# A graph-attention and three-layer GCN kernel: GpSimd waits once per attention batch, ahead of its third group of four row gathers

## The chip, the cores and the metric

The kernel runs on one core of one Trainium2 chip. The metric is the device time of one execution in microseconds (us), and a smaller number is better. Before the change it is 5381.48 us, the median of three runs.

## What is computed

The graph has 6250 nodes with 128 features and 106,250 edges, sorted by destination. Everything is float32. First comes one heterogeneous graph-attention layer with 8 heads of 16 features, 4 node types and 6 edge types. Cut to what matters here:

```python
k, q, v = (typed_linear(x, W, ntype) for W in (Wk, Wq, Wv))     # by node type
kw = typed_rel(k[src], rel_att, etype)                          # by edge type
a  = (kw * q[dst]).sum(-1) * rel_pri.T[etype] / sqrt(16)
m  = typed_rel(v[src], rel_msg, etype)
ex = exp(a - segment_max(a, dst)[dst])
h  = segment_sum(m * (ex / segment_sum(ex, dst)[dst]), dst)     # then Wa, gate, layer norm
```

Three GCN layers follow, each of which sums h[src] * norm over the edges of a destination, with a batch norm behind it, and a last residual and layer norm.

## The kernel before

**Tables.** Because the key and message of an edge depend only on its source node and its edge type, the kernel first writes a table `kv_tab` to HBM with one row per node and edge type: 37,500 rows of 256 floats (1 KB), the key half and the message half. This takes the first 420 us or so.

**Attention batches.** The edges are then handled in 52 batches (`NB`) of 16 tiles (`TPB`) of 128 edges. A batch has four groups (`NG`) of four tiles (`GRP`). GpSimd fetches the rows of a tile with one indirect DMA, `G.indirect_dma_start(kv[b % 3][:, t, :], ...)` at L528, which brings 128 rows of 1 KB (128 KB). So a batch takes 16 gathers, issued one behind the other by the loop in `gather(b)`. The rows land in one of three buffers, `kv[b % 3]`, and each group of four gathers has its own semaphore, `kv_land[b % 3][g]`, which is at 64 * (b // 3 + 1) when all four have landed.

The work on a batch is spread over the engines, written out in a fixed order by hand:

- TensorE takes the query rows of each tile by a one-hot matrix product (`q_rows`, L866; it signals `q_done` per group). For the batch one behind it, it runs a few tiny products that carry the segment maximum from tile to tile (`chain_f` L890, `spread_f` L894, `chain_b` L898, `spread_b` L902), and the weighted sums over the edges of a tile (`aggregate`, L881 and L884).
- VectorE multiplies keys and queries (`products`, L1228, which waits for `kv_land` and for `q_done`), reduces them to logits (L1235), runs the scans of the segment maximum (`max_1` to `max_5`; L1264 is the first instruction of `max_2` and waits for `chain_f`; L1269 waits for `spread_f`), multiplies messages and weights (`weigh`, L1307, which signals `vw_ready` per group), and adds the sums of TensorE to the accumulators in SBUF (L1330).
- ScalarE builds the one-hot matrices (L646, L650, L658, L661; L646 waits for `q_done` of a group two back) and takes the exponentials.
- In each of batches 1 to 34 SyncE also writes two or three blocks of zeros of 1.8 MB into a dense matrix `a_tab` in HBM (`feed`, L423), at the time of the gathers of the batch one further on.

**What paces GpSimd.** The rows of batch b take the place of batch b - 3. So `gather(b)` waits, group by group, for `vw_ready` of batch b - 3: `pool.wait_ge(vw_ready, NG * (b - 3) + g + 1)`. TensorE, VectorE and ScalarE are working on batch b - 1 or b - 2 at that time. Besides the gathers GpSimd issues scatters of single words into `a_tab` (`scatter`, L485), which are spread over the batches by `slots`: none in some, two in others, and nine in each batch from number 37 on. From batch 3 on each batch therefore shows as one burst of GpSimd DMAs. Behind the last batch GpSimd issues 48 more scatters in a row (`SY`).

**GCN layers.** In each layer GpSimd gathers rows of 512 bytes (L557) in groups of four into a ring of four groups, and before a group it waits for `sum_done`, a signal of TensorE's sums (L998), while TensorE multiplies the dense part (L1021).

Of the kernel before, what the change touches and what calls it, by code (L numbers as in the profile page):

```python
# [62 lines left out]
def gnn(nc, x, src, dst, etype, ew, ntype, Wk, Wq, Wv, Wa, rel_pri, rel_att, rel_msg, skip, gamma, beta,  # L63
# [50 lines left out]
    with ExitStack() as ctx:  # L114
# [3 lines left out]
        def sem(name):  # L118
            return ctx.enter_context(nc.semaphore(name))
# [137 lines left out]
        kv_land = [[sem(f"kv_land{a}_{g}") for g in range(NG)] for a in range(3)]  # L257
# [199 lines left out]
        def _(pool):  # L457
# [26 lines left out]
            def scatter(t):  # L484
                G.indirect_dma_start(a_tab, bass.IndirectOffsetOnAxis(cell[:, t:t + 1], 0), tot[:, t:t + 1], None)\  # L485
                 .then_inc(cells_saved, 16)
# [17 lines left out]
            for j in range(ZC - 1, NCH - 1):  # L504
                b = 2 if j < ZC else next(b for b in range(NB) if zeros_by(b) >= BPC * (j + 1)) + 3
# [8 lines left out]
            def gather(b):  # L514
                pool.wait_ge(idx_ready, b + 1)
                pool.sem_inc(gathers_begun, 1)
                if b == 2:
                    pool.wait_ge(tot_ready, 1)
                for g in range(NG):
                    for t, j in slots.get((b, g), ()):  # L520
                        pool.wait_ge(a_zeroed[j], 16 * BPC)
                        scatter(t)
                    if b >= 3:
                        pool.wait_ge(vw_ready, NG * (b - 3) + g + 1)
                        pool.sem_inc(gathers_begun, 1)
                    for s in range(GRP):
                        t = g * GRP + s
                        G.indirect_dma_start(kv[b % 3][:, t, :], None, kv_tab,  # L528
                                             bass.IndirectOffsetOnAxis(idxr[:, b % 3, t:t + 1], 0))\
                         .then_inc(kv_land[b % 3][g], 16)  # L530
            for b in range(NB):
                gather(b)
# [1098 lines left out]
```

## Time and profile before

| | |
|---|---|
| time, median of three runs | 5381.48 us (5376.69 to 5386.73) |
| the profiled execution: span from first to last instruction | 5345.2 us, 57754 instructions |
| the profiled execution's own time | not listed; the median of the runs is 36.3 us above its span |
| busy share PE / PEld / DVE / ACT / POOL | 72% / 49% / 44% / 21% / 49% |
| attention batches, start of the gathers to start of the last burst | 422.8 to 2555.7 us |
| mean granted TensorE clock | 0.832 of full speed |
| gathers of attention: POOL L528 | x832, 808.5 us busy, mean 972 ns |
| before them POOL idle | 889.4 us, 64 times, on DVE L1307 |

How to read it: times are microseconds from the first instruction. PE is TensorE's matmuls, PEld its weight loads, DVE VectorE, ACT ScalarE, POOL GpSimd, SP SyncE; POOL's span of an indirect DMA is the time in which it makes the descriptors, not the time in which the rows move. In a row of the timeline the bracket holds the time for which the engine sat idle before the instruction, and what ended it. "remote" is an event that the profile can't put to an instruction that has just ended, and "issue" is idle time in which the engine waited for nothing that the profile shows.

### The profile page before, as it was taken

Reading aid. Unit: us, or ns where it says so; the run is one execution under the profiler, and the core shown is the slowest. Engines: PE = TensorE matmul, PEld = TensorE weight load, DVE = VectorE, ACT = ScalarE, POOL = GpSimd, SP = SyncE. Lnnn points to the kernel's source line nnn. Section 1 sums busy time; section 2 is a strip of 40 time slices with the busy share of each in tenths; the row PEclk is TensorE's granted clock in tenths of the full one; section 3 lists DMA queues with packets and bytes.
Section 4 is the critical chain, followed back from the end, with each engine's and each line's share of the span. In section 5 each row is a group of like instructions: output and inputs, shape, how many; then the busy total and the mean of one; then the engine's idle time right before and its main releaser. Section 6 shows DMA issues by size and latency. Waiting matters only on the chain. (4 is left out here: it accounts for less than half of the span.)

```text
span 5345.2 us, 57754 instructions
## 1 busy us (share of the span) xinstructions
PE 3871.6 (72%) x17006; PEld 2627.4 (49%) x17006; DVE 2374.6 (44%) x8260; ACT 1139.1 (21%) x2513; POOL 2613.5 (49%) x2753
## 2 busy tenths in 40 slices
PE   5883666666666655555362889999889899889996
PEld 4662555555555544444330544444544445445453
DVE  4552444444544433433264354334454335454336
ACT  1222444544444433333211100000000000000001
POOL 0004344344443455445533466665566665666663
PEclk9996777776777666666575999999999999999998
DMA  7994445444454322112001566767677677767774
GB/s 170 380 396 152 181 156 182 145 172 166 148 188 147 106 61 59 56 52 63 22 25 55 204 252 260 273 254 273 254 261 266 254 268 265 265 252 267 269 268 153
DMA packets 265570, 1020.69 MB, mean 191 GB/s; under 512 B 66086, under 2 KB 114373, under 8 KB 227632
## 3 DMA queue, kind: packets, MB, share of 16 engines
q1 hardware_dynamic: 132060, 716.86, 35.7%
q0 software_dynamic: 102352, 248.59, 14.4%
q10 hardware_dynamic: 30852, 51.55, 2.8%
q8 instruction: 145, 2.38, 0.2%
q14 instruction: 161, 1.32, 0.1%
HBM read 797.16 MB, written 219.61 MB: 190 GB/s over the span
## 5 line engine op out<-in xcount | busy, mean ns | idle before, releaser
L557 POOL DMA_INDIRECT stage<-h_tab,earr x1536 | 1454.3, 947 | 879.9 <-issue 425.1
L1021 PE MATMUL bank<-arena,xr 128*128 128x512 f32 (+1 forms) x3822 | 1748.3, 600 | 57.6 <-issue 54.6
L528 POOL DMA_INDIRECT arena<-kv_tab,idxr x832 | 808.5, 972 | 1161.1 <-DVE arena L1307 889.4
L1021 PEld LDWEIGHTS bank<-arena,xr 128*128 128x128 f32 x3822 | 707.8, 194 | 808.3 <-issue 808.0
L1540 DVE TENSOR_TENSOR sums<-sums,bank 128x128 f32 x1536 | 437.2, 285 | 907.2 <-remote 706.4
L881 PE MATMUL bank<-oh,stage 128*128 128x128 f32 x1664 | 408.7, 371 | 341.2 <-issue 337.2
L1511 DVE TENSOR_SCALAR oh<-iota_j,earr 128x128 f32<-128x128 f32 x1536 | 557.6, 370 | 96.8 <-DVE sums L1531 29.8
L998 PEld LDWEIGHTS bank<-oh,stage 128*128 128x128 f32 x3072 | 398.2, 193 | 333.1 <-issue 332.2
L881 PEld LDWEIGHTS bank<-oh,stage 128*128 128x128 f32 x1664 | 338.4, 272 | 423.7 <-issue 422.1
L884 PE MATMUL bank<-oh,arena 128*128 128x128 f32 x1664 | 380.3, 367 | 196.2 <-issue 189.0
L646 ACT ACTIVATE arena<-arena,iota_p 128x512 f32<-128x512 bf16 x416 | 276.2, 712 | 1137.8 <-remote 1049.0
L866 PE MATMUL bank<-xr,arena 128*128 x3328 | 460.6, 300 | 69.3 <-issue 40.7
L998 PE MATMUL bank<-oh,stage 128*128 128x128 f32 x3072 | 424.1, 280 | 113.7 <-issue 112.5
L712 ACT ACTIVATE rs<-mv,epsc 128x49 f32<-128x49 f32 (+1 forms) x6 | 1.9, 316 | 2314.8 <-DVE mv L1583 2120.9
L866 PEld LDWEIGHTS bank<-xr,arena 128*128 128x128 f32 x3328 | 443.6, 216 | 75.5 <-issue 74.1
L884 PEld LDWEIGHTS bank<-oh,arena 128*128 128x128 f32 x1664 | 326.3, 272 | 224.5 <-issue 224.4
L1330 DVE TENSOR_TENSOR sums<-sums,bank 128x256 f32 x832 | 347.8, 418 | 57.0 <-DVE sums L1330 11.8
L485 POOL DMA_INDIRECT a_tab<-tot,cell x320 | 310.4, 970 | 100.1 <-issue 99.8
L1228 DVE TENSOR_TENSOR arena<-arena,bank 128x512 f32<-128x512 f32 x208 | 142.3, 684 | 486.1 <-remote 408.0
L658 ACT ACTIVATE oh<-iota_j,earr 128x128 f32<-128x128 f32 x832 | 262.6, 386 | 57.8 <-remote 52.6
L1264 DVE COPY negall<-bank 8x16 f32<-8x16 f32 x52 | 8.4, 162 | 599.5 <-remote 576.0
L650 ACT ACTIVATE arena<-arena,epsc 128x512 f32<-128x512 f32 x416 | 274.6, 708 | 0.0
(217 smaller groups left out, 2887.6 us busy)
## 6 DMA issues: line engine op xcount, KB each, us to landing
arena<-a_tab SPq DMA_DIRECT2D x273, 1792.0 KB
a_tab<-stage SPq DMA_DIRECT2D x70, 1792.0 KB
a_tab<-sums POOLq DMA_DIRECT2D x21, 1792.0 KB, 13.4
kv_tab<-stage SPq DMA_DIRECT2D x48, 768.0 KB
arena<-rel_d SPq DMA_DIRECT2D x52, 512.0 KB
stage<-h_tab,earr POOLq DMA_INDIRECT x1536
arena<-key_d ACTq DMA_DIRECT2D x40, 512.0 KB, 10.7
arena<-in_edge_weight ACTq DMA_DIRECT2D x40, 512.0 KB, 13.4
```

Of the source, the lines that this page charges most:

```text
L485: G.indirect_dma_start(a_tab, bass.IndirectOffsetOnAxis(cell[:, t:t + 1], 0), tot[:, t:t + 1], None)\
L528: G.indirect_dma_start(kv[b % 3][:, t, :], None, kv_tab, bass.IndirectOffsetOnAxis(idxr[:, b % 3, t:t + 1], 0))\
L557: G.indirect_dma_start(gring[:, (q % NG) * GRP + s, :], None, h_tab[l], bass.IndirectOffsetOnAxis(src_i[:, t:t + 1], 0)).then_inc(row_land ...
L646: al.inc(S.activation(ohT[k][:, g % 2, :], relb[:, par, g * GRP * P:(g + 1) * GRP * P], ACT.Abs, scale=-1.0, bias=iota_p[:, k:k + 1]))
L866: last = M.matmul(bank[g % 2][:, s * D:(s + 1) * D], ohT[k][:, g % 2, s * P:(s + 1) * P], xr[:, k:NT - 1 + k, :][:, bass.ds(blocks[s], 1), ...
L881: M.matmul(o_[s][:, P:2 * P], exw[:, g * GRP + s, :], oh[:, g, s, :], start=True, stop=True)
L884: last = M.matmul(o_[s][:, 0:P], vw[:, g * GRP + s, :], oh[:, g, s, :], start=True, stop=True)
L998: last = M.matmul(bank[q % NG][:, s * P:(s + 1) * P], gring[:, (q % NG) * GRP + s, :], oh[:, q % NG, s, :], start=True, stop=True)
L1021: mm = M.matmul(o_[:, 0:cw], xr[:, n, :], abuf[B % NBUF][:, n % KB, 0:cw], start=n == 0, stop=n == NT - 1)
L1330: V.tensor_tensor(w_, w_, d_.rearrange("p (k j) -> p k j", k=2), ALU.add).then_inc(acc_added, 1)
L1511: V.tensor_scalar(oh[:, q % NG, s, :], iota_j[:, :], rel_c[:, t:t + 1], ew_c[:, t:t + 1], ALU.is_equal, ALU.mult).then_inc(wt_ready, 1)
L1540: V.tensor_tensor(w_, w_, bank[q % NG][:, s * P:(s + 1) * P], ALU.add).then_inc(win_added, 1)
```

## The change

One wait is added in `gather(b)`, on GpSimd. In every batch, when it comes to the third group of gathers (g == 2), GpSimd waits until the four gathers of the second group of the same batch have landed. The wait stands ahead of the scatters and of the `vw_ready` wait of that group. All instructions, their order and their sizes stay as they are.

```diff
@@ -517,6 +517,8 @@
                 if b == 2:
                     pool.wait_ge(tot_ready, 1)
                 for g in range(NG):
+                    if g == 2:
+                        pool.wait_ge(kv_land[b % 3][g - 1], 64 * (b // 3 + 1))
                     for t, j in slots.get((b, g), ()):
                         pool.wait_ge(a_zeroed[j], 16 * BPC)
                         scatter(t)
```

## Rows read from the trace of the kernel before

**Rows 1.** Page, part 2: DMA share in 40 slices of the span.
```profile
DMA  7994445444454322112001566767677677767774
```

**Rows 2.** Waits, 515 to 2606 us: total us, times, longest us.
```profile
ACT arena L646 <- remote: 992.3, 91, 21.4
POOL arena L528 <- DVE arena L1307: 889.4, 64, 29.9
DVE negall L1264 <- remote: 502.7, 43, 21.0
...
PEld bank L881 <- issue: 417.6, 468, 2.7
```

**Rows 3.** Timeline of POOL: starts (and two ends) of bursts; start, us.
```profile
515.05 0.94 POOL L528 DMA_INDIRECT arena<-kv_tab,idxr  x1 [29.89 <-DVE arena L1307]
...
594.33 0.94 POOL L528 DMA_INDIRECT arena<-kv_tab,idxr  x1 [18.41 <-DVE arena L1307]
632.21 0.94 POOL L528 DMA_INDIRECT arena<-kv_tab,idxr  x1 [17.81 <-DVE arena L1307]
...
1700.29 0.94 POOL L528 DMA_INDIRECT arena<-kv_tab,idxr  x1 [17.72 <-DVE arena L1307]
...
1722.02 0.95 POOL L528 DMA_INDIRECT arena<-kv_tab,idxr  x1 [0.30 <-issue]
1740.91 0.94 POOL L528 DMA_INDIRECT arena<-kv_tab,idxr  x1 [17.94 <-DVE arena L1307]
...
2063.96 0.99 POOL L528 DMA_INDIRECT arena<-kv_tab,idxr  x1 [16.95 <-DVE arena L1307]
...
2094.76 0.96 POOL L485 DMA_INDIRECT a_tab<-tot,cell  x1 [0.30 <-issue]
...
2113.37 0.99 POOL L528 DMA_INDIRECT arena<-kv_tab,idxr  x1 [17.65 <-DVE arena L1307]
...
2555.68 0.99 POOL L528 DMA_INDIRECT arena<-kv_tab,idxr  x1 [17.48 <-DVE arena L1307]
```

**Rows 4.** Timeline of the batch whose burst starts at 1700.29.
```profile
1704.57 3.65 PEld L866 LDWEIGHTS bank<-xr,arena 128*128 128x128 f32 x32
...
1714.75 0.69 DVE L1228 TENSOR_TENSOR arena<-arena,bank 128x512 f32<-128x512 f32 x1 [7.39 <-remote]
...
1726.17 0.16 DVE L1264 COPY negall<-bank 8x16 f32<-8x16 f32 x1 [9.80 <-remote]
...
1731.80 0.18 DVE L1269 TENSOR_TENSOR tmp<-bank,tsel 128x16 f32<-128x16 f32 x1 [3.31 <-PE bank L894]
...
1733.67 0.23 PE L898 MATMUL bank<-rhs,hsel 128*8 128x32 f32 x2
```

**Rows 5.** Timeline of the first burst, batches 0 to 2.
```profile
431.60 0.95 POOL L528 DMA_INDIRECT arena<-kv_tab,idxr  x1 [0.30 <-issue]
...
439.37 0.69 DVE L1228 TENSOR_TENSOR arena<-arena,bank 128x512 f32<-128x512 f32 x1 [2.46 <-DMA arena<-kv_tab,idxr]
...
441.02 2.05 PE L866 MATMUL bank<-xr,arena 128*128 x16 [0.37 <-issue]
...
473.37 1.33 ACT L646 ACTIVATE arena<-arena,iota_p 128x512 f32<-128x512 bf16 x2 [36.02 <-remote]
```

**Rows 6.** Timeline of the last batches, VectorE, no gathers left.
```profile
2662.25 1.29 DVE L1307 TENSOR_TENSOR arena<-arena,stage 128x512 f32<-128x512 f32 x2 [0.17 <-ACT stage L677]
...
2685.17 1.29 DVE L1307 TENSOR_TENSOR arena<-arena,stage 128x512 f32<-128x512 f32 x2 [0.16 <-ACT stage L677]
```

**Rows 7.** Timeline of POOL in a GCN layer, behind twelve gathers.
```profile
3513.63 0.94 POOL L557 DMA_INDIRECT stage<-h_tab,earr  x1 [2.57 <-remote]
```

**Rows 8.** Windows, two bursts: us, busy PE, PEld, DVE, ACT, POOL; PEclk, DMA share, GB/s.
```profile
1700.29:1722.96 22.67, 12.53 (x80) 11.37 (x79) 7.99 (x20) 6.04 (x11) 17.49 (x18) 0.73 0.77 276
...
2063.96:2095.72 31.76, 15.02 (x86) 12.82 (x85) 7.96 (x20) 5.84 (x11) 24.45 (x25) 0.66 0.30 87
```

**Rows 9.** Waits of POOL: total us, times, longest us.
```profile
POOL stage L557 <- remote: 291.9, 125, 3.8
```

## The prediction

> **What bounds the kernel now.** I read the slices of the page first. The attention batches fill the stretch from about 423 to 2700 us, and there no engine and no DMA queue is full: the DMA share is 0.4 to 0.5 while zeros are written and 0.1 to 0.2 later [rows 1]. So some chain of waits must set the pace, and the list of waits names its members: ScalarE, VectorE and GpSimd all wait, and TensorE's L881 sits idle 468 times in front of one instruction on "issue" [rows 2].
>
> The timeline of GpSimd shows the pattern. Each batch is a burst of DMAs 1.25 us apart and then some 18 us in which GpSimd waits for `weigh`. The length of a batch is burst plus a constant. A batch with 16 DMAs takes 632.21 - 594.33 = 37.9 us, one with 18 takes 40.6 us, one with 25 takes 49.4 us [rows 3]: 9 more DMAs at 1.28 us make 11.5 us more, all of it paid. Yet the gathers are for a batch that nobody needs soon. So the burst is serial with the attention work, although no data ties them.
>
> The timeline of one batch shows where. The query products (L866, begun at 1704.57, half of them done by 1706.5) free L1228 and L646 only at 1714.7. L1264 is let go only at 1726.17, which is 3.2 us behind the end of the burst (1722.97) [rows 3, 4]. The first burst, of three batches, is plainer: the products at 437 to 440.7 let ScalarE go at 473.37, with TensorE empty in between [rows 5]. What TensorE has done becomes visible late while GpSimd issues DMAs back to back, and TensorE itself then steps on in single instructions. Bandwidth is not the reason: in the burst at 2063.96 the DMA share is 0.30, in the one at 1700.29 it is 0.77, and the constant behind the burst is about the same, 17.65 and 17.94 us [rows 3, 8]. Without GpSimd's DMAs a batch takes 2685.17 - 2662.25 = 22.9 us [rows 6]. I call this the backlog, without a claim on what it consists of. It begins some 6 us into a burst (the products of 1704.57 are the first work caught) and ends some 3 us behind its end. Which part of the chip does it, these rows do not tell.
>
> The page "TensorE: Matmul & The Clock Gate" of the Trainium skill (the paragraph on engine queue depths) gives TensorE a queue of 64 instructions. By that rule work could run ahead by 64 before TensorE itself stumbles, and the trace has it get through the 32 loads and 32 products of L866 at full speed first [rows 4]. Nothing below needs this.
>
> **The change, part by part.** It adds one wait, no instruction with a duration, and moves nothing in order. Queued behind it on GpSimd are the scatters and eight gathers of groups 2 and 3 (11.3 us in an 18-DMA batch) and then the next batch; who waits for those is `products` of two batches on, which has over a period of slack, so the late landing of groups 2 and 3 costs nothing (the cover is some 40 us, the delay under 7). SyncE's queue is not touched.
>
> The pause, step one, its price. GpSimd's own pause costs g', the landing time of group 1 less the 0.3 us of idle that stands before a gather anyway. No wait of this kind is in the trace. From below: in the GCN layers a pause between two gathers lasts 2.57 - 0.30 = 2.3 us by its row [rows 7]; it ends with a signal of TensorE, not with a landing. The mean of 125 such pauses is 291.9 / 125 = 2.3 us with those 0.3 in it [rows 9], so 2.0 us is the lower end. From above: the second group of the very first batch was issued by 432.55 and its rows were seen at 439.37 [rows 5], 6.8 us, so 6.5 us, with 1.8 MB blocks of zeros ahead of it in GpSimd's own queue. In the bursts with SyncE's zeros (batches 3 to 35, 33 of them) I take 4.0 us, between the ends, since those zeros are in another queue. In the 15 further periods the DMA share is 0.30 [rows 8] and I take 2.0 us, with 2.9 us as the upper end (the 3.2 us from a burst's end to the release of L1264, less 0.3).
>
> "DMA: Bandwidth & Descriptors" of the Trainium skill ("Anatomy of one DMA") gives a GpSimd DMA about 2.0 us plus bytes over 436 GB/s, which would be 2.3 us for 128 KB; an estimate by that page would be a g' of 2.0 us throughout.
>
> Step two, what the pause frees. Behind it the backlog should end, as it ends behind each burst, and what TensorE had done by then becomes visible: L1228, and some 2 us later L1264 (my estimate: L1228 itself and two like it stand before it, 0.7 us each [rows 4]). From there the chain runs at full speed, until GpSimd has again issued for some 6 us. L1264 to L1269 takes 1731.80 - 1726.17 = 5.6 us [rows 4], with 2 us before it 7.6 us, so I expect the backlog of the second half to catch the release of L1269. It is held until 3.2 us behind the end of the second half. What is then left to the next burst is 1740.91 - 1731.80 = 9.1 us, where now it is 1740.91 - 1726.17 = 14.7 us [rows 3, 4]. A batch was 22.7 + 3.2 + 14.7 = 40.6 us; it will be 22.7 + g' + 3.2 + 9.1, a change of g' - 5.6 us.
>
> Sum: 33 x (4.0 - 5.6) = -52.8 us and 15 x (2.0 - 5.6) = -54 us, together -106.8 us. The first burst and the last one, with its 48 scatters, pay a pause and win a little; I put them at nothing (within 5 us). The GCN layers are not touched. The span goes from 5345.2 to 5238 us, and with the 36.3 us by which the median of the runs stands above it, the time to 5275 us, 2.0% less. With the upper g' in all, the change is 33 x 0.9 - 15 x 2.7 = -11 us; with the lower one 48 x -3.6 = -173 us. So this case reaches from 5208 to 5371 us.
>
> **The rivals.**
> A, slower: the pause does not clear the backlog. The place is the restart of GpSimd. All pauses that I see end with a signal of TensorE, that is after the state has ended; the new one ends with a DMA, and may end sooner. Then L1264 still waits for the end of the whole burst and the pause comes on top: 33 x 4.0 + 15 x 2.0 = +162 us, 5543 us (48 x 2.0 = +96 us, 5477 us, to 33 x 6.5 + 15 x 2.9 = +258 us, 5639 us). It decides where g' is shorter than what ends the state, some 3 us, or g' above 5.6 us for any reason. For it: 2.0 is under 3. Against it: a burst's end and a landing are nearly one event, and the first half has the zeros to make g' longer.
>
> "Rules for kernel authors" on that page, "DMA: Bandwidth & Descriptors" of the Trainium skill, say to issue DMAs early and wait on their semaphore late, so that the fixed cost overlaps. The wait here stands right behind the issue; by that rule nothing is won and each pause is exposed. No run here shows it yet.
>
> B, no change: the two cancel, when g' is near its upper end in the zeroing batches. 5370 to 5392 us.
>
> C, more: the backlog of the second half comes later, or the chain gets there sooner. If L1269 passes and L898's result (1733.67, 2.1 us later with 7.2 us left [rows 4]) is the first caught, each batch wins 1.9 us more: 48 x 1.9 = 91 us, 5184 us, with the low g' 5117 us. If nothing of the second half is caught, a batch is 11.3 us (first half) + 3 + 2 + 14.7 = 31.0 us in place of 40.6: 48 x -9.6 = -461 us, 4920 us. For it: a second half of 8 gathers is 10 us, of which only 4 are slow. Against it: in the bursts now, work done 6 us in was already 8 us late [rows 4].
>
> **How the numbers follow.** Main case 0.50 (of it 0.01 within the bound of no change), A 0.20, B 0.07, C with L898 0.15, C in full 0.08. A measurement of this kernel can tell 0.2% (11 us) from no change: the three runs lie within 10 us. Faster 0.49 + 0.15 + 0.08 = 0.72, same 0.01 + 0.07 = 0.08, slower 0.20. The predicted time is that of the main case, 5275 us; its own range is 5208 to 5371 us. For 8 in 10 the range takes in the lower C and B, and the near edge of A: 5110 to 5480 us (0.50 + 0.15 + 0.07 + some 0.06). Outside are the full C and most of A.
>
> **What would show it.** In the timeline of POOL each burst falls in two halves of 8 gathers, with an idle of 2.3 to 7 us between them put down to a DMA or to remote; its mean over 52 batches is g' + 0.3. If the main case holds, L1264 sits some 15 us behind the start of the burst and no longer 3 us behind its end, its wait of 502.7 us [rows 2] falls to under 250 us, a new wait of 5 us or more stands before L1269, and GpSimd's wait for L1307 falls from 17.7 to about 12 us. If L1264 stays 3 us behind the burst's end and GpSimd's wait stays at 17.7, it is A. If bursts follow each other in 31 us, it is C in full. The prediction is wrong in its base if the backlog hangs on something other than GpSimd's back-to-back issue, for instance on how many DMAs a batch has in all.

## The result and the profile after

The changed kernel takes 5132.88 us, the median of four runs (5121.71 to 5159.32). The kernel before, timed beside it, takes 5379.08 us (5375.12 to 5386.73). The ratio is 0.9548, 95% interval 0.9521 to 0.9576: 246 us less, where 106 us less was forecast. The direction was right and the time lies in the range of 5110 to 5480 us, near its lower end and below the main case's own range of 5208 to 5371 us.

The profiled execution of after has a span of 5120.0 us and took 5121.71 us, so a time is its span and 1.7 us. The 36.3 us which the forecast put around the span of before were therefore not around it: that profiled execution took about 5347 us, less than each of the four runs timed beside after. A second profile of the kernel before, taken later, has a span of 5379.4 us.

Lines that stand behind the new wait have moved by two: L528 is L530 now, L1264 is L1266, L1269 is L1271, L1307 is L1309. The page of after:

```profile
PE 3800.9 (74%) x17006; PEld 2582.1 (50%) x17006; DVE 2370.9 (46%) x8260; ACT 1140.0 (22%) x2513; POOL 2613.6 (51%) x2753
...
L530 POOL DMA_INDIRECT arena<-kv_tab,idxr x832 | 809.0, 972 | 889.2 <-DVE arena L1309 396.0
```

and the gathers on the page of before:

```profile
L528 POOL DMA_INDIRECT arena<-kv_tab,idxr x832 | 808.5, 972 | 1161.1 <-DVE arena L1307 889.4
```

The work is the same as before, and the gathers take as long as they did. All idle time in front of them fell from 1161.1 to 889.2 us, 271.9 us less. The part of it spent on `weigh` (L1307, now L1309) fell from 889.4 to 396.0 us, and a part of what was saved there is taken by the new wait.

The attention batches in two windows, first of after and then of before. Columns: us, then busy us and instructions of PE, PEld, DVE, ACT, POOL, then the granted clock, DMA share and GB/s. The first window of each holds the 33 periods with SyncE's zeros (batches 3 to 35), the second the 15 behind them:

```profile
507.63:1628.54 1120.91, 747.13 (x4687) 686.04 (x4687) 609.92 (x1651) 607.85 (x1354) 550.07 (x567) 0.78 0.55 192
1628.54:2311.57 683.03, 403.19 (x2132) 358.94 (x2132) 277.25 (x751) 279.19 (x616) 364.73 (x374) 0.68 0.21 61
```
```profile
515.05:1819.75 1304.70, 820.51 (x4688) 740.34 (x4688) 608.47 (x1651) 609.44 (x1354) 549.50 (x567) 0.72 0.46 165
1819.75:2555.68 735.93, 400.94 (x2132) 348.10 (x2132) 276.12 (x751) 276.59 (x616) 364.76 (x374) 0.67 0.20 57
```

The 33 zeroing periods went from 1304.70 / 33 = 39.54 us to 1120.91 / 33 = 33.97 us, 5.6 us each and 183.8 us in all. The 15 others went from 49.06 to 45.54 us, 3.5 us each and 52.9 us in all. The start of batch 3 comes 7.4 us sooner. What lies behind the start of the last burst is 5120.0 - 2311.57 = 2808.4 us long against 5345.2 - 2555.68 = 2789.5 us, 18.9 us more. So 183.8 + 52.9 + 7.4 - 18.9 = 225.2 us, which is the difference of the spans. The 18.9 us are no effect of the change: in a second pair of profiles, both from one chip (Q below), the last part is 2802.1 us after and 2810.7 us before. On that pair the periods went from 39.58 to 33.99 us and from 49.69 to 46.22 us, again 5.6 and 3.5 us.

Waits of after, 500 to 2460 us: total us, times, longest us.

```profile
ACT arena L648 <- remote: 500.4, 52, 21.3
POOL arena L530 <- DVE arena L1309: 396.0, 57, 18.6
...
DVE tmp L1271 <- remote: 220.1, 16, 58.2
POOL arena L530 <- DMA arena<-kv_tab,idxr: 202.8, 29, 7.7
...
DVE negall L1266 <- remote: 125.8, 18, 14.3
```

ScalarE's wait for TensorE has halved from 992.3 us, and VectorE's wait at L1266 (L1264 before) is down from 502.7 to 125.8 us [rows 2]. The new wait shows as a DMA that lets L530 go: 29 times, 202.8 / 29 = 7.0 us each. Where a scatter stands first behind it, it is put down to L485 instead, and where it is short, to "issue".

One late batch of after, POOL first and then VectorE:

```profile
2129.26 0.99 POOL L530 DMA_INDIRECT arena<-kv_tab,idxr  x1 [12.14 <-DVE arena L1309]
...
2141.00 0.94 POOL L530 DMA_INDIRECT arena<-kv_tab,idxr  x1 [0.30 <-issue]
2144.00 0.97 POOL L485 DMA_INDIRECT a_tab<-tot,cell  x1 [2.06 <-DMA arena<-kv_tab,idxr]
...
2161.81 0.95 POOL L485 DMA_INDIRECT a_tab<-tot,cell  x1 [0.30 <-issue]
2174.87 0.99 POOL L530 DMA_INDIRECT arena<-kv_tab,idxr  x1 [12.10 <-DVE arena L1309]
...
2143.85 0.69 DVE L1230 TENSOR_TENSOR arena<-arena,bank 128x512 f32<-128x512 f32 x1 [7.56 <-remote]
...
2165.69 0.17 DVE L1271 TENSOR_TENSOR tmp<-bank,tsel 128x16 f32<-128x16 f32 x1 [13.57 <-remote]
```

The last gather of the first half ends at 2141.94 and L1230, which waited since 2136.3 for products that TensorE had ended by 2137.8, is let go at 2143.85, 1.9 us later and inside the pause. The second half then catches what L1271 waits for; it comes at 2165.69, 2.9 us behind the end of the burst, and 9.2 us later GpSimd may start again.

One zeroing batch of after, in the same order:

```profile
1495.92 0.94 POOL L530 DMA_INDIRECT arena<-kv_tab,idxr  x1 [6.76 <-DVE arena L1309]
...
1505.05 0.95 POOL L530 DMA_INDIRECT arena<-kv_tab,idxr  x1 [0.30 <-issue]
1512.83 0.94 POOL L530 DMA_INDIRECT arena<-kv_tab,idxr  x1 [6.84 <-DMA arena<-kv_tab,idxr]
...
1529.54 0.94 POOL L530 DMA_INDIRECT arena<-kv_tab,idxr  x1 [7.01 <-DVE arena L1309]
...
1507.71 0.69 DVE L1230 TENSOR_TENSOR arena<-arena,bank 128x512 f32<-128x512 f32 x1 [4.73 <-remote]
...
1509.24 0.15 DVE L1266 COPY negall<-bank 8x16 f32<-8x16 f32 x1
...
1514.55 0.17 DVE L1271 TENSOR_TENSOR tmp<-bank,tsel 128x16 f32<-128x16 f32 x1 [3.00 <-PE bank L896]
...
1523.56 0.14 DVE L1286 COPY sx<-sx 8x1 f32<-8x1 f32 x1 [5.75 <-remote]
```

Here the pause is 6.84 us, but the backlog ends 1.7 us into it (1506.00 to 1507.71). For the other 5 us the chain runs at full speed. It passes L1266 without a wait and L1271 with the normal one for `spread_f`, and is caught only at L1286, which leaves 1529.54 - 1523.56 = 6.0 us to the next burst. The batches scatter, from 28.1 to 41.1 us. In 28 of the 33 the pause is 6.8 to 7.7 us, and they take 33.2 us in the mean; in five it is only 2.6 us, and these take 38.2 us. These five come each right behind a batch of 28.2 to 28.4 us, and GpSimd had waited at most 1.5 us before them, so the short pause and the long period can't be told from the payback of a very fast batch. VectorE's waits from 515 to 1640 us say what is caught how often:

```profile
DVE arena L1230 <- remote: 166.6, 30, 6.4
DVE sx L1286 <- remote: 96.0, 18, 8.0
DVE sums L1332 <- remote: 55.2, 8, 10.1
...
DVE negall L1266 <- remote: 20.4, 3, 7.8
```

and the same for the late batches, 1660 to 2320 us:

```profile
DVE tmp L1271 <- remote: 153.6, 13, 16.4
DVE negall L1266 <- remote: 103.1, 14, 14.3
```

### The profile page after: what moved, and what is told of

Read it like the earlier page. It is cut to its first block and busy times, and to the rows that moved or that the text cites. A ratio compares the mean times of both kernels' runs of the same rounds, so it can differ in the third digit from the quotient of the medians.

```text
span 5120.0 us, 57770 instructions
## 1 busy us (share of the span) xinstructions
PE 3800.9 (74%) x17006; PEld 2582.1 (50%) x17006; DVE 2370.9 (46%) x8260; ACT 1140.0 (22%) x2513; POOL 2613.6 (51%) x2753
## 5 line engine op out<-in xcount | busy, mean ns | idle before, releaser
L530 POOL DMA_INDIRECT arena<-kv_tab,idxr x832 | 809.0, 972 | 889.2 <-DVE arena L1309 396.0
L868 PE MATMUL bank<-xr,arena 128*128 x3328 | 501.3, 302 | 209.1 <-issue 169.9
L868 PEld LDWEIGHTS bank<-xr,arena 128*128 128x128 f32 x3328 | 457.7, 214 | 239.9 <-issue 238.2
L1000 PEld LDWEIGHTS bank<-oh,stage 128*128 128x128 f32 x3072 | 397.9, 192 | 355.0 <-issue 353.5
L1000 PE MATMUL bank<-oh,stage 128*128 128x128 f32 x3072 | 426.8, 280 | 133.1 <-issue 131.9
L883 PE MATMUL bank<-oh,stage 128*128 128x128 f32 x1664 | 360.5, 366 | 135.4 <-issue 126.8
L648 ACT ACTIVATE arena<-arena,iota_p 128x512 f32<-128x512 bf16 x416 | 275.6, 710 | 564.4 <-remote 535.9
L1332 DVE TENSOR_TENSOR sums<-sums,bank 128x256 f32 x832 | 347.4, 418 | 111.9 <-remote 55.2
L883 PEld LDWEIGHTS bank<-oh,stage 128*128 128x128 f32 x1664 | 311.4, 270 | 160.6 <-issue 157.3
L485 POOL DMA_INDIRECT a_tab<-tot,cell x320 | 310.0, 969 | 128.7 <-issue 97.5
L886 PE MATMUL bank<-oh,arena 128*128 128x128 f32 x1664 | 317.1, 343 | 49.2 <-issue 47.8
L886 PEld LDWEIGHTS bank<-oh,arena 128*128 128x128 f32 x1664 | 291.0, 256 | 72.1 <-issue 72.0
L1230 DVE TENSOR_TENSOR arena<-arena,bank 128x512 f32<-128x512 f32 x208 | 142.1, 683 | 316.2 <-remote 289.5
L1533 DVE TENSOR_TENSOR sums<-sums,stage 128x1 f32 x960 | 154.9, 161 | 253.3 <-issue 65.6
```

The source lines that it names most:

```text
L530: G.indirect_dma_start(kv[b % 3][:, t, :], None, kv_tab, bass.IndirectOffsetOnAxis(idxr[:, b % 3, t:t + 1], 0))\
L648: al.inc(S.activation(ohT[k][:, g % 2, :], relb[:, par, g * GRP * P:(g + 1) * GRP * P], ACT.Abs, scale=-1.0, bias=iota_p[:, k:k + 1]))
L868: last = M.matmul(bank[g % 2][:, s * D:(s + 1) * D], ohT[k][:, g % 2, s * P:(s + 1) * P], xr[:, k:NT - 1 + k, :][:, bass.ds(blocks[s], 1), ...
L883: M.matmul(o_[s][:, P:2 * P], exw[:, g * GRP + s, :], oh[:, g, s, :], start=True, stop=True)
L886: last = M.matmul(o_[s][:, 0:P], vw[:, g * GRP + s, :], oh[:, g, s, :], start=True, stop=True)
L1000: last = M.matmul(bank[q % NG][:, s * P:(s + 1) * P], gring[:, (q % NG) * GRP + s, :], oh[:, q % NG, s, :], start=True, stop=True)
```

## The experiments

Here P, Q, R and S are names for four chips. In the tables "early" is the mean period of the 33 zeroing batches and "late" that of the 15 behind them, both read from the starts of the bursts as above. A ratio is against the kernel before on the same chip. The diffs are against the changed kernel. The kernel before takes 5344 and 5351 us on P, 5378 us on Q, 4115.0 us on R and 4115.7 us on S. Which chip the main result comes from is not on record. The runs beside it (5375 to 5387 us) are like those of Q (5374 to 5386 us). The first profile of before is like P: its 5347 us lie within P's times (5337 to 5356 us), and its periods of 39.54 and 49.06 us and last part of 2789.5 us are those of group0 there (39.47, 49.05 and 2786.7 us), where Q has 39.58, 49.69 and 2810.7 us.

### On chip P: is it the pause, and which part of it?

**group0** waits for the first group's rows, which have landed by then; **every** waits ahead of each of the groups 1 to 3.

```diff
-                        pool.wait_ge(kv_land[b % 3][g - 1], 64 * (b // 3 + 1))
+                        pool.wait_ge(kv_land[b % 3][0], 64 * (b // 3 + 1))
```
```diff
-                    if g == 2:
+                    if g >= 1:
```

> The wait ahead of the third group asks for the rows of the first group in place of the second. Theory 1 (back-to-back issue on GpSimd holds back TensorE's results, and a pause frees them): the first group has been issued 5 us earlier and has landed by then in most batches, so there is hardly a pause (0.3 us of idle ahead of the third group in the 25-DMA batches, 0 to 2 us in the batches with zero blocks), the 25-DMA batches take 49.4 us again, and the time is 5340 to 5385 us. Theory 2 (what counts is that some earlier rows are known to have landed, whatever the pause): 5133 us as with the change.

> The same wait ahead of the second, third and fourth group: three pauses in a batch. Theory 1: GpSimd never issues for more than 5 us (7.7 us with scatters) without a pause, so little is ever held back; a batch comes down to what the attention work takes (23 to 31 us) or to GpSimd's own 31.8 + 3 x 2 = 38 us in the 25-DMA batches; some 31 us in 33 batches and 38.5 us in 15: time about 4930 us. Rival (the pauses are a price, and one of them has already won what there is): two more pauses of 2 us in 15 batches and of 4 us in 33 come on top, 5133 + 60 + 264 = 5460 us.

**pad_short** and **pad_long** have no wait for rows: GpSimd writes zeros four or thirteen times into a part of SBUF that nobody uses at that time, work that the kernel doesn't need.

```diff
-                        pool.wait_ge(kv_land[b % 3][g - 1], 64 * (b // 3 + 1))
+                        for _ in range(4):
+                            link.link(G.memset(nodes[:, 0:512], 0.0))
```

> No wait for rows; ahead of the third group GpSimd instead fills an unused tile four times, about 2.3 us without a DMA issue. Theory 1: the break in issuing is what frees the results, so the 25-DMA batches take 45.6 us as with the change, and the batches with zero blocks, whose pause falls from 7.1 to some 2.5 us, take 34 to 35 us: 5120 to 5180 us in all. Rival (the rows must have landed, as they had after 7 us in those batches): these 33 batches lose their gain and pay the 2.3 us, 5380 to 5450 us.

> As the short fill, with thirteen fills, about 7.5 us without a DMA issue in every batch. Theory 1 with the free run (during a longer pause the chain of the batch goes on, so its length is no price): 25-DMA batches at 43 to 46 us, the others at 33 to 35 us, 5100 to 5150 us. Rival (every us of pause past the release is a price): 15 x 5.4 us more, 5215 us or above.

| kernel | time us | ratio, 95% | early | late |
|---|---|---|---|---|
| group0 | 5336.12 | 0.9981 (0.9972 to 0.9991) | 39.47 | 49.05 |
| every | 4931.32 | 0.9221 (0.9206 to 0.9237) | 33.22 | 37.58 |
| pad_short | 5070.65 | 0.9478 (0.9463 to 0.9494) | 35.03 | 42.54 |
| pad_long | 5099.66 | 0.9533 (0.9516 to 0.9549) | 34.80 | 44.35 |

Waits of POOL in group0, 515 to 1500 us:

```profile
POOL arena L530 <- DVE arena L1309: 449.3, 36, 18.5
...
POOL arena L530 <- DMA arena<-kv_tab,idxr: 0.3, 1, 0.3
```

With the wait in place but nothing to wait for, there is no pause and the periods are those of before. So it is the pause that wins. The two fills show that it needs no landing and no idle engine: in pad_short GpSimd goes on working, and its DMA issue breaks off for 2.56 us where a scatter follows the fill, as in the late batches, and for 3.10 us where a gather follows, as in the early ones. A late batch of it:

```profile
2143.74 0.95 POOL L531 DMA_INDIRECT arena<-kv_tab,idxr  x1 [0.30 <-issue]
2144.67 2.30 POOL L522 MEMSET nodes<- 128x512 f32 x4
2146.40 1.33 ACT L649 ACTIVATE arena<-arena,iota_p 128x512 f32<-128x512 bf16 x2 [10.97 <-remote]
...
2147.25 0.99 POOL L485 DMA_INDIRECT a_tab<-tot,cell  x1 [0.28 <-POOL nodes L522]
```

ScalarE is let go at 2146.40, 1.7 us behind the last issue (2144.69) and in the middle of the fill. No rows have to land for it and GpSimd need not rest. The early batches say the same more plainly: in all 33 VectorE's products are let go 1.6 to 2.1 us behind the last issue, while rows take some 7.5 us to land at that place (the pauses ahead of the third group in every). What ends the backlog is the break in the issue of DMAs. In six of the 15 late batches the products were let go within 0.4 us, too soon for the break to be the reason.

Early the length hardly counts. pad_long breaks for 8.35 us early and 7.8 us late, 5.2 us longer than pad_short, and the early periods are the same within 0.3 us; the late ones are 1.8 us longer, a third of what the break is longer. The rival of pad_long, that each microsecond is a price, fails. What the length does move is the instruction that is caught. VectorE's waits of pad_short and then of pad_long, 520 to 1660 us (L1272 is L1269 of before, L1333 the sums, L1330 of before):

```profile
DVE tmp L1272 <- remote: 298.0, 31, 10.5
```
```profile
DVE sums L1333 <- remote: 163.9, 18, 12.9
DVE tmp L1272 <- remote: 135.8, 15, 16.3
```

In every, the list of waits of VectorE from 515 to 1640 us, and of POOL from 515 to 1500 us, have a new head:

```profile
DVE arena L1230 <- DMA arena<-kv_tab,idxr: 302.3, 67, 9.0
```
```profile
POOL arena L530 <- DMA arena<-kv_tab,idxr: 282.0, 52, 8.8
```

The chain is held less, but GpSimd's burst with its three pauses now fills the period: no burst from batch 3 on waits for `weigh` any more, and VectorE waits for rows. The pauses have gone from a cure to the bound; a shorter break should be better. The time is the 4930 us that was expected; pad_short came out 49 us below its range.

### On chip P: long pauses, a part of the batches, and shorter breaks

**zeros_early** has all of SyncE's zeros written by batch 12 or so, so that batches 13 to 35 have the pause without them. **late_only** pauses only from batch 36 on (`SB`).

```diff
-    zeros_by = lambda b: min(NBLK, BPC * ZC + (3 * b if b < 3 else 2 * b + 3))
+    zeros_by = lambda b: min(NBLK, BPC * ZC + 8 * b)
```
```diff
-                    if g == 2:
+                    if g == 2 and b >= SB:
```

> The change, with SyncE's blocks of zeros written eight to a batch in batches 1 to 9 in place of two to a batch in 1 to 34 (the scatters that need them move with them). From batch 12 to 35 a batch then has 16 gathers, the pause and no zeros. Theory 1 (it is the long pause, 7 us under the zeros, in which the chain runs on past L1269's release): without zeros the pause is 2.05 us, VectorE is caught at L1269's counterpart again, and the gain per batch falls from 5.6 us to the 3.8 us of the late batches, 37.9 - 3.8 = 34.1 us a batch. Rival (16-DMA batches gain more whatever the pause): 32.3 us a batch or less.

> The wait only in batches 36 to 51. Theory 1 (each batch's gain is its own): the period of these falls by 3.6 us as with the change, that of batches 3 to 35 stays at 39.5 us, the sum is -55 us of the before time, ratio 0.990. Rival (a batch gains because its neighbour's burst has changed): 15 x less than 2 us, ratio 0.995 or above.

**pad_every4** and **pad_every2** have the fill ahead of each of the groups 1 to 3, four or two times, and no wait for rows.

```diff
-                    if g == 2:
-                        pool.wait_ge(kv_land[b % 3][g - 1], 64 * (b // 3 + 1))
+                    if g >= 1:
+                        for _ in range(2):
+                            link.link(G.memset(nodes[:, 0:512], 0.0))
```

> Four fills (2.56 us without a DMA issue) ahead of the second, third and fourth group, no wait for rows. Theory 1: the results are let go in each pause, and the pauses under the zeros are 2.56 us in place of 4.1 us, so GpSimd's bound falls from 33.2 to 20.3 + 7.7 = 28 us in 33 batches, and stays near 39 us in the late ones: some 28 to 30 us early, ratio 0.89 to 0.90. Rival (rows not landed is what holds the results back under the zeros): early batches at 36 us or more, ratio 0.94 or above.

> Two fills (about 1.3 us without a DMA issue) at the same three places. Theory 1 with a threshold (in the traces TensorE's results come 1.7 to 1.9 us behind the last issue): a pause of 1.3 us frees nothing, and the three add up as a price, 3 x 1.3 = 3.9 us in each of 48 batches, ratio 1.03. Rival (each us without issue counts the same, wherever it lies): half of what the 2.56 us pauses give, ratio 0.94 to 0.95.

| kernel | time us | ratio, 95% | early | late |
|---|---|---|---|---|
| zeros_early | 5135.40 (one run) | – | 36.11 | 43.93 |
| late_only | 5272.27 | 0.9857 (0.9841 to 0.9874) | 39.54 | 43.91 |
| pad_every4 | 4831.49 | 0.9029 (0.9014 to 0.9044) | 29.67 | 38.98 |
| pad_every2 | 4826.95 | 0.9015 (0.8994 to 0.9036) | 28.34 | 40.47 |

A batch of 16 gathers in zeros_early, behind the zeros; second half, next start, and VectorE:

```profile
1310.40 0.94 POOL L530 DMA_INDIRECT arena<-kv_tab,idxr  x1 [2.54 <-DMA arena<-kv_tab,idxr]
...
1331.04 0.94 POOL L530 DMA_INDIRECT arena<-kv_tab,idxr  x1 [10.94 <-DVE arena L1309]
...
1355.32 0.17 DVE L1271 TENSOR_TENSOR tmp<-bank,tsel 128x16 f32<-128x16 f32 x1 [8.42 <-remote]
```

Without zeros the pause is 2.5 us in place of 6.8 us, and the chain is caught at L1271 again, as in the late batches. Batches 13 to 35 have 16 DMAs each now and take 33.2 us in the mean. The ten of these batches that have 16 DMAs in the other kernels too take 37.9 us before and 31.8 us in after. So the break alone wins 4.7 us, and with the zeros, where most pauses are 4 us longer, 6.1 us. The other 1.4 us, with a scatter of some 4 us from batch to batch, are not shown to be the length's: in the same ten batches the 8.35 us of pad_long (33.7 us) win no more than the 3.10 us of pad_short (33.1 us). Most of the win needs only the break.

late_only leaves the early periods at 39.54 us, as before to the hundredth, and wins 5.1 us in each late one, more than the 3.6 us expected from the change; zeros_early has 43.93 us there too. The pause is the same as in after, 2.1 us, so on P a late batch wins more than on Q (3.5 us). The batches are independent in this: each pays and wins for itself.

Two fills do as well as four, and both expectations of pad_every2 (1.03, and 0.94 to 0.95) missed. How long the break is depends on what follows the fill: a scatter comes 0.3 us behind it, a gather 0.8 us. A break of pad_every2 ahead of a gather, where the gather before ended at 1016.92:

```profile
1016.92 1.12 POOL L522 MEMSET nodes<- 128x512 f32 x2
1018.85 0.95 POOL L531 DMA_INDIRECT arena<-kv_tab,idxr  x1 [0.81 <-POOL nodes L522]
```

It is 1.93 us, and 1.40 us where a scatter follows. The mean of its breaks is 1.75 us early and 1.45 us late; for four fills it is 2.9 and 2.6 us. The early batches prefer the shorter break (28.34 against 29.67 us), the late ones the longer (38.98 against 40.47 us). In the late batches the breaks are shorter than the 1.6 to 2.1 us that the release in a single long break takes, and the periods still fall from 49.05 to 40.47 us. So a break need not last as long as such a release, as I had supposed for pad_every2.

### Chips R and Q: one fill, the mix, and a chip without backlog

**every1** has one fill (a break of 0.82 us ahead of a scatter and 1.35 us ahead of a gather, 1.16 us early and 0.86 us late in the mean) ahead of the groups 1 to 3; **mix** two in batches below `SB` and three from there on; **mix_gcn** is mix and four fills ahead of every second group of gathers in the GCN layers; **pairs1** has a single fill behind each second gather, seven in a batch.

```diff
+            def fill(n):
+                for _ in range(n):
+                    link.link(G.memset(arena[:, at - 512:at], 0.0))
...
-                    if g == 2:
-                        pool.wait_ge(kv_land[b % 3][g - 1], 64 * (b // 3 + 1))
+                    if g >= 1:
+                        fill(2 if b < SB else 3)
```

(`fill(1)` in every1.) In mix_gcn also

```diff
+                    if q % 2:
+                        for _ in range(4):
+                            link.link(G.memset(gmask[:, :, :], 0.0))
```

and in pairs1, ahead of each gather and without the fill above,

```diff
+                        if s == 2 or g and not s:
+                            fill(1)
```

> One fill ahead of the second, third and fourth group: some 0.8 us without a DMA issue (0.5 us more than the usual 0.3 us), three times a batch. Theory 3 (back-to-back issue builds up something that drains only in a break of a certain length, somewhere under 1.4 us as two fills showed): 0.8 us is too short or just enough; if too short, the batches keep the 39.5 and 49.1 us of before plus 1.6 us, ratio 1.01. Rival (it drains in proportion to the idle time): 0.55 of what two fills won, ratio 0.945.

> Two fills ahead of each of the three groups in batches 0 to 35 and three in batches 36 to 51. By the periods of the two runs with two and four fills everywhere (28.3 us early with two; 40.5 with two and 39.0 with four late) the early part takes 28.3 us a batch and the late part 38 to 40 us: ratio 0.895 to 0.902, the fastest version so far. If three fills late fare no better than two: 0.902.

> As mix, and in the GCN layers some 1.5 us of fills ahead of every second group of four gathers as well. Theory 1 carried over (TensorE's sums are seen late there too, VectorE waits 706 us for them before the change): the breaks free them and TensorE's stalls at the end of each run of 12 gathers go; GpSimd's own time rises by 192 x 1.5 = 290 us, which fits its 290 us of waits for sums: 0.01 to 0.03 less ratio than mix. Rival (TensorE's 0.9 busy share bounds these layers and GpSimd's queue becomes the longer): same as mix or up to 0.02 more.

> One fill of some 0.5 us ahead of every second gather, seven in a batch: about the same time without issue as two fills at three places (3.7 against 3.3 us), but in pieces of 0.8 us. Theory 3 (a break has to have a certain length): little or nothing won, ratio 0.98 to 1.02. Rival (the mean rate of issue counts): as two fills at three places, ratio 0.90 to 0.92.

| kernel, chip R (before 4115.02) | time us | ratio, 95% | early | late |
|---|---|---|---|---|
| every1 | 4196.39 | 1.0193 (1.0173 to 1.0213) | – | – |
| mix | 4317.21 | 1.0488 (1.0469 to 1.0508) | 26.32 | 37.38 |
| mix_gcn | 4492.74 | 1.0913 (1.0892 to 1.0934) | – | – |
| pairs1 | 4267.44 | 1.0371 (1.0350 to 1.0391) | 25.58 | 35.61 |

All four missed, and all on the same side. On this chip the kernel before itself takes 4115 us, 1260 us less than on Q, so the wins expected for the other chips could not be had here. The kernels were run again, before and after among them, on chip Q, and the last two on chip S.

> The kernel before, unchanged. If its time is 5340 to 5390 us: bursts and 17.7 us of wait as in the first profile. If it is about 4115 us, theory 4 (on that chip TensorE's results are not held back): GpSimd issues the bursts with no wait for L1307 between them, 20.3 us a batch with 16 DMAs and 31.8 us with 25, the last burst starts near 1700 us, and VectorE has no long waits on remote. Rival (the attention is as before and something else, such as the clock in the GCN layers, is faster): batches of 39.5 and 49.1 us again.

> The change, unchanged. On a chip with before at 5340 to 5390 us: ratio 0.950 to 0.960. On a chip with before at 4115 us, theory 4: the pause is only a price to a GpSimd that is the bound, 33 batches of 6.8 us (less if other things wait anyway) and 16 of 1.8 us: +250 us, ratio 1.06; rival: 0.96 as elsewhere.

> Two fills ahead of three groups early, three fills late. With before at 5340 to 5390 us: ratio 0.895 to 0.902, as put down the first time. With before at 4115 us: 1.049 as measured there, since the pauses add 3.3 us to 33 batches and about 5 us to 16.

> One fill (0.8 us without issue) ahead of three groups. With before at 5340 to 5390 us: 1.01 if a break has to be longer than that, 0.945 if idle time counts in proportion. With before at 4115 us: 1.019 as measured there.

> One fill ahead of every second gather, seven breaks of 0.8 us in a batch. With before at 5340 to 5390 us: if the idle time counts in proportion (one fill at three places adds 3 x 0.5 us of break and won 0.046, two add 3 x 1.1 us and won 0.099), seven such breaks win 0.09 to 0.11, ratio 0.89 to 0.91; if a break has to be long, it is 0.954 or above. With before at 4115 us: 1.037 as measured there.

> Mix plus 1.5 us of fills ahead of every second group in the GCN layers. With before at 5340 to 5390 us: if TensorE is held back there too and breaks free it, 0.87 to 0.89, where mix alone gave 0.896; if GpSimd's longer queue costs what it frees, 0.896 to 0.92. With before at 4115 us: 1.091 as measured there.

| kernel | chip | time us | ratio, 95% | early | late |
|---|---|---|---|---|---|
| before_again | Q | 5381.17 | – | 39.58 | 49.69 |
| after_again | Q | 5128.44 | 0.9540 (0.9524 to 0.9556) | 33.99 | 46.22 |
| mix_again | Q | 4823.53 | 0.8960 (0.8943 to 0.8977) | 29.09 | 37.81 |
| every1_again | Q | 5130.53 | 0.9537 (0.9521 to 0.9553) | 33.50 | 47.12 |
| pairs1_again | S | 4270.45 | 1.0377 (1.0360 to 1.0395) | – | – |
| mix_gcn_again | S | 4492.03 | 1.0912 (1.0894 to 1.0930) | – | – |

On Q every1 met neither of its two expected ratios (1.01 and 0.945) but came near the second: breaks of about 1 us win 6.1 us in an early batch, more than the change does, and 2.6 us in a late one.

The same kernel, mix, gives both ratios. Its waits on chip R, 520 to 1900 us, and then on chip Q, same window:

```profile
DVE arena L1234 <- DMA arena<-kv_tab,idxr: 316.6, 75, 7.5
...
ACT arena L652 <- PE bank L872: 139.7, 46, 4.4
```
```profile
ACT arena L652 <- remote: 221.0, 28, 20.1
...
DVE negall L1270 <- remote: 166.0, 33, 14.2
DVE sums L1336 <- remote: 137.8, 32, 9.5
```

On R the head of the list is a DMA, and ScalarE is let go by TensorE's own instruction as it ends. On Q more of the same waits end with "remote", that is with an event that the profile can't put to an instruction that has just ended. In the GCN layers, 2400 to 4200 us, the wait for TensorE's sums shows the same, R and then Q:

```profile
DVE sums L1546 <- PE bank L1004: 626.0, 238, 16.1
```
```profile
DVE sums L1546 <- remote: 480.2, 85, 18.7
POOL stage L563 <- remote: 224.8, 89, 3.9
```

On R no such hold shows, and most of what the fills add is paid. By the traces mix adds 36 x 3 breaks that are 1.45 us longer than the usual 0.3 us, and 16 x 3 that are 1.74 us longer, 240 us; it took 202 us more. every1 adds 36 x 3 x 0.86 + 16 x 3 x 0.56 = 120 us and took 81 us more. pairs1 adds 52 x 7 x 0.5 = 182 us and took 152 us more. The fills in the GCN layers cost another 176 us (mix_gcn against mix). GpSimd is the bound of the attention part on R: in mix there no burst from batch 3 on waits for `weigh`, on Q 17 of 49 do. The change itself did not run on R or S; an estimate from its mean pauses on the chip of the main result, 6.46 us early and 2.09 us late, less 0.3 each, is up to 33 x 6.2 + 16 x 1.8 = 233 us more than 4115 us.

Most of what still sets the chips apart lies behind the attention. With mix, Q takes 511 us more than R in the profiled executions; up to the start of the last burst it is 105 us (2026.94 against 1922.16), and behind it 406 us (2799.5 against 2393.1). There mix leaves Q about where before had it (2810.7 us).

## Why the prediction was right in its direction and short in its size

**The backlog, and that a pause ends it: held.** group0 removes the pause and keeps the instruction, and the win is gone (0.998). pad_short keeps the break and removes the landing, and the win stays (0.948). The rival A, that the pause doesn't clear it, is refuted by the timeline as well: in 42 of the 48 batches L1230 waits when the pause begins, and it is let go 1.2 to 2.1 us behind the last issue, inside the pause each time, if once by only 0.02 us (the shortest pause is 1.96 us). Without a pause the same wait, L1228 of before, ends 3.1 to 7.9 us behind that gather in 29 of the 33 zeroing batches. The reason given for A was that a burst's end needs some 3 us; that was the time to L1264's release and not to the first one.

**The late batches: the sum held, in part by luck.** Forecast: a pause of 2.0 us net, the catch at L1269 held until 3.2 us behind the burst, 9.1 us left, 15 x -3.6 = -54 us. Measured: 1.8 us net, L1271 (the old L1269) at 2.9 us, 9.2 us left, 15 x -3.5 = -52.9 us. GpSimd's wait for `weigh` is 12.1 us where 12 was named. But the 5.6 us that the pause frees were read from a zeroing batch. In the late batch of before whose burst ends at 2095.72, L1264 is let go 3.9 us behind the burst and not 3.2 us, with 13.8 us left to the next burst and not 14.7 us:

```profile
2099.61 0.16 DVE L1264 COPY negall<-bank 8x16 f32<-8x16 f32 x1 [18.84 <-remote]
```

So 1.0 us came from an earlier release and 4.6 us from what is left, together again 5.6 us. The -52.9 us also set a profile of after beside one of before that looks like chip P. Within Q it is 15 x -3.5 = -52 us, but on P, by late_only, 15 x -5.1 = -77 us.

**The zeroing batches: this is the step that failed.** "So I expect the backlog of the second half to catch the release of L1269", with 9.1 us left, and g' = 4.0 us, gave 33 x (4.0 - 5.6) = -53 us. Measured are 33 x -5.6 = -184 us, and these 131 us are nearly all of the miss (most of the rest is the 7 us ahead of batch 3). By the forecast's own condition for rival A, g' above 5.6 us, these batches should even have lost, 33 x 0.6 = 20 us; that they won is not to the forecast's credit. Two things of it were off, of opposite sign. The price of the pause was too low: 6.46 us in the mean of the 33 (five are short), 6.2 us net, near the upper end. And what it frees, step two, was taken as fixed at 5.6 us, though it hangs on the pause's length: I let the chain start with the end of the pause, while it starts 1.7 to 2.1 us into it. A long pause is mostly time in which the chain runs. For the batch at 1495.92 my formula says 20.1 (16 DMAs) + 4.0 + 3.2 + 9.1 = 36.4 us; measured are 20.1 + 6.5 + 1.0 + 6.0 = 33.6 us. The longer pause cost 2.5 us more, the release came 2.2 us sooner behind the burst, and the later catch left 3.1 us less. Over the 33 batches the catch lies at L1286 18 times and at L1332 8 times. This is the place of rival C, one step further than the main case; I had given it 1.9 us more and 15%. pad_short and pad_long show the same on one chip, with nothing but the length changed: a break of 3.10 us has L1269's counterpart caught in 31 early batches, one of 8.35 us in 15, with the sums caught 18 times, and the win is 4.5 and 4.7 us. So a longer pause pays for itself, and no more. Why the landing wait on Q wins 5.6 us, about 1 us more than either fill on P, stays open.

The mean granted clock of the early window also rose, from 0.72 to 0.78; what share of the 5.6 us is that, no run separates.

zeros_early tests the account. With a pause of 2.5 to 3.9 us the catch is at L1271 again in most batches, as the main case had it, and the win is 4.7 us. For the batch at 1331.04 the terms are 20.1 + 2.4 + 1.8 + 9.2 = 33.4 us (its burst ends at 1353.54, L1271 comes at 1355.32, the next burst at 1364.48). Only the release differs from the formula, 1.8 us behind the burst in place of 3.2 us.

**The rule against it.** "DMA: Bandwidth & Descriptors" of the Trainium skill, in its rules for kernel authors, has DMAs issued early and their semaphore waited on late. On chip Q the runs disagree: the wait right behind the issue makes the kernel 4.6% faster (0.9540). No wait for a landing ran on R or S. In "Anatomy of one DMA" the same page of the Trainium skill gives about 2.0 us and the bytes over 436 GB/s, an estimate of 2.3 us for 128 KB. It is near the late pauses (2.06 us) and those of zeros_early (2.5 us), and far from those beside SyncE's zeros (6.84 us); there the measurement decides.

**The base.** No run shows the 36.3 us as time around the span; what the runs show is 1.7 us. The first profile of before most likely comes from another chip than the runs timed, though the record doesn't say so. The forecast is not moved by it, since I had added them to reach the median.

**What stays open.** Which part of the chip holds TensorE's results back, and what sets chips P and Q apart from R and S, no run here tells. Also open is whether the spread breaks of pairs1 or the breaks in the GCN layers help where there is a backlog, since both ran only on R and S. The GCN part of mix has such waits on Q, 480.2 us at L1546 between 2400 and 4200 us. Of the kernels run, the best on Q is mix, 4823.5 us (0.896), and on R and S the one before.

## What to carry to other kernels

When many engines wait for "remote" while one issues DMAs back to back, and all are let go a fixed time behind its last issue, break the issue up; it need not be a wait for data, three breaks of 1.4 to 1.9 us in a batch won 10% on chip P, where the one landing wait won 4.6% on Q. When a pause is put in, ask what runs during it: its price is its length less what the waiting chain gains inside it, and the chain starts when the hold ends, not when the pause does. Time the kernel before on every chip on which a version is judged, since the sign hangs on it: mix is 10.4% faster on Q and 4.9% slower on R.

## What the runs showed of the hardware

- While GpSimd issues DMAs back to back, ScalarE and VectorE see TensorE's results late on P and Q. In a break they come 1.6 to 2.1 us behind the last issue in all 33 early batches of pad_short, where GpSimd writes zeros (2144.69 to 2146.40 for ScalarE in a late one), and 1.2 to 2.1 us in after, where it idles (1506.00 to 1507.64 for ScalarE's L648); in before, without a break, 3.1 to 7.9 us behind the same gather.
- Breaks in the issue ahead of three groups, early and late mean, give these ratios: 1.16 and 0.86 us 0.954 (every1 on Q), 1.75 and 1.45 us 0.902 and 2.9 and 2.6 us 0.903 (pad_every2 and pad_every4 on P).
- Behind a fill a scatter starts 0.3 us later and a gather 0.8 us later (1.40 and 1.93 us of break in pad_every2).
- A gather's rows land with a pause of 2.06 us when little else moves, and with 6.84 us beside SyncE's writes of zeros (6.8 to 7.7 us in 28 of 33 batches).
- The same kernel before takes 5344 to 5378 us on two chips and 4115 us on two others, with the two of each pair within 0.7% of each other; on the latter 68 to 84% of the time that breaks add is paid.
